# One-hot lookups in every stage of a factor-interaction tower, clears of scratch between gathers, and batches of four units

## The chip, the cores and the metric

The kernel runs on one core of one Trainium2 chip. The metric is the device time of one execution in microseconds (us); lower is better. All data are float32, the ids int32.

## What is computed

A batch of 1024 rows has 32 fields; field f of a row picks a row of 64 numbers from its table. For every pair of fields (p, q) a 64x64 matrix is applied to the first and the product is summed against the second, which gives 496 features. They go, with 16 dense ones, through three layers.

```python
e = jnp.stack([tbl_0[ids[:, 0]], ..., tbl_31[ids[:, 31]]], axis=1)   # 1024 x 32 x 64
p, q = e[:, ROW], e[:, COL]                                          # 496 pairs
kp = jnp.einsum('bpj,ipj->bpi', p, kernel)
z = jnp.sum(kp * q, axis=-1)
h = jnp.concatenate([z, dense_ctx], axis=1)
h = jnp.maximum(h @ W_top1 + b_top1, 0.0)      # 512
h = jnp.maximum(h @ W_top2 + b_top2, 0.0)      # 256
y = h @ W_top3
```

Thirteen of the tables have 1000 rows; the others have 1250, 12500 or 125000.

## The kernel before

Everything is held with the 64 numbers of two fields (a **group**, 16 of them) on the 128 partitions and batch rows on the columns. The batch is worked in four **stages** of 256 rows. A stage has 124 slots of four pairs each (`SLOT`), and two slots are a **unit**: 62 units in a stage, 248 in all. Per unit

- TensorE does four matmuls of 256 columns (`products`, L535) into one of three PSUM buffers `kp`, with the constants in `k_sb`;
- VectorE multiplies the result with the second factor (L481 in one instruction of 1024 columns, or L491 in two of 512) into a ring `prod` of 12 units;
- TensorE sums over partitions with selector matmuls of 32 output rows (`reductions`, L552). They are done per **batch** of units: batches are 5, 6 and 5 units long (`BATCH_UNITS`), and batch b is summed after the fourth unit of batch b+1 (`LAG`).

The groups reach the chip so: GpSimd gathers 128 rows of one table with one indirect DMA (L375); four of them fill one buffer `raw` (a ring of four), two transposes of 128x128 (L519) turn it and ScalarE copies the result from `tr_ps` to `pair` (L393). One such step is an **event**; there are 16 in a stage and 64 in all, and the table `TRANSPOSE_AT` says before which unit each stands in TensorE's program. GpSimd may fill a buffer again when its transposes are done.

Groups 0, 2 and 4 of the first stage are not gathered. Their tables have 1000 rows, so a row is found by a **one-hot lookup**: the table lies on 125 partitions with 8 rows each, VectorE compares the ids, sent to all partitions, with the row numbers (L464, 16 instructions of 256 columns per group), and TensorE multiplies table and one-hot matrix (L511, 16 matmuls of 256 columns per group). The one-hot matrices lie in `prod`, the tables in the end of `k_sb`, which `kd` fills later (L321).

SyncE issues the loads in program order (`load_hot_ids` L332, `load_tables` L338, `load_k` L321) and the copies between partition halves (L329). The loads of the last layers come in the fourth stage. After unit 247 TensorE does the three layers (L573, L579, L586).

In the program each float32 matmul is one instruction; in the trace it is two records with a weight load each, so that a row "x40" is 20 matmuls.

Of the kernel before, what the change touches and what calls it, by code (L numbers as in the profile page):

```python
# [5 lines left out]
I32 = mybir.dt.int32  # L6
# [5 lines left out]
P = 128  # L12
# [13 lines left out]
PROD_RING = 12  # L26
LAG = 4
# [8 lines left out]
BATCH_UNITS = (5, 6, 5)  # L36
# [71 lines left out]
LOOKUP = (0, 2, 4)  # L108
SMALL = 1000
SMALL_P, SMALL_C = 125, 8  # L110
HOT_UNITS = 2 * SMALL_C * WIDTH // (2 * ROWS)

# [7 lines left out]
def unit_slots(u):  # L120
    return range(UNIT[u][1], UNIT[u][1] + UNIT_SLOTS)
# [83 lines left out]
TRANSPOSE_AT = [0, 0, 0, 1, 2, 3, 7, 9, 13, 15, 20, 23, 25, 31, 36, 41, 43, 47, 52, 57, 61, 62, 66, 71, 74, 77, 82,  # L205
                87, 90, 93, 98, 103, 105, 109, 114, 119, 123, 124, 128, 133, 136, 139, 144, 149, 152, 155, 160, 165,
                167, 171, 176, 181, 185, 186, 190, 195, 198, 201, 206, 211, 214, 217, 222, 227]
assert len(TRANSPOSE_AT) == len(EVENT)
assert all(TRANSPOSE_AT[group_event(UNIT[u][0], g)] <= u
           for u in range(UNITS) for s in unit_slots(u) for tile in SLOT[s] for g in groups_of(tile))  # L210

# [20 lines left out]
def pairwise_tower(nc, dense, ids, hot_ids, row_no, tables, kd, ident_in, sel_in, w1, b1, w2, b2, w3, out):  # L232
    from contextlib import ExitStack
    ctx = ExitStack()
    with ctx:
# [3 lines left out]
        def sem(name):  # L239
# [9 lines left out]
        hot_ids_sb = sb("hot_ids_sb", [P, len(LOOKUP), 2, WIDTH], I32)  # L249
# [31 lines left out]
        ids_in = sem("ids_in")  # L281
        consts_in = sem("consts_in")
        row_no_in = sem("row_no_in")
        hot_ids_in = [sem(f"hot_ids_in{i}") for i in range(len(LOOKUP))]
        table_in = [sem(f"table_in{i}") for i in range(len(LOOKUP))]
# [32 lines left out]
        def _(sp):  # L318
# [22 lines left out]
            sp.dma_start(row_sb[0:SMALL_P, :], row_no).then_inc(row_no_in, 16)  # L341
# [6 lines left out]
            for j in range(1, K_AHEAD):  # L348
                load_k(j)
            for u in range(UNITS):  # L350
                st, s = UNIT[u]
                for m in fours_at(u):
                    mix_across(st, m)
                j = s // K_LOAD
# [88 lines left out]
        def _(dve):  # L443
# [14 lines left out]

            dve.wait_ge(row_no_in, 16)
            for i in range(len(LOOKUP)):  # L460
                dve.wait_ge(hot_ids_in[i], 16)
                for c in range(SMALL_C):
                    for n in range(2):
                        nc.vector.tensor_scalar(hot(i, n, c), hot_ids_sb[0:SMALL_P, i, n, :],  # L464
                                                row_sb[0:SMALL_P, c:c + 1], None,
                                                ALU.is_equal).then_inc(hot_ready, 1)
            for u in range(UNITS):
                st, s = UNIT[u]
                if u < PROD_RING and u % HOT_UNITS == 0:

                    dve.wait_ge(transposed, group_event(0, LOOKUP[u // HOT_UNITS]) + 1)
# [14 lines left out]
                else:  # L486
# [7 lines left out]
                    last.then_inc(prod_done, 1)  # L494
            add_dense(LAST)

        @block.tensor
        def _(pe):
            pe.wait_ge(consts_in, 2 * 16)

            def transpose_event(e):
# [169 lines left out]
```

## Time and profile before

| | |
|---|---|
| Time, median of 3 runs | 451.96 us (451.67 to 453.82) |
| Profiled execution: time | 451.3 us |
| Profiled execution: span of its trace | 449.5 us |
| Granted TensorE clock, mean | 0.996 |
| Busy in the span: PE (matmul) | 428.2 us (95%) |
| PEld (weight load) | 283.0 us (63%) |
| DVE (VectorE) | 302.9 us (67%) |
| ACT (ScalarE) | 70.5 us (16%) |
| POOL (GpSimd) | 230.5 us (51%) |

Span is the time from the first to the last instruction of the trace. PE and PEld are the two sides of TensorE. A start time is counted from the start of the span. A chain ("chain that ended last") is followed back from the last instruction, at each step to what released it or to the instruction before it on its engine.

### The profile page before, as it was taken

To read this page: it belongs to the slowest core of one execution; us is meant where nothing else is said; L and a number is where in the kernel's file an instruction comes from. 1 tells how busy PE (TensorE), PEld (TensorE's weight loads), DVE (VectorE), ACT (ScalarE), POOL (GpSimd) and SP (SyncE) were. 2 spreads that over 40 slices of the span, in tenths; PEclk is the share of its full clock that TensorE was granted. 3 is DMA by queue.
4 is the path that set the end of the run, shared out by engine and by line. 5 is a ranking of instruction groups with operands and counts; after the bars stand their busy time and mean duration, and the time that the engine had idled before them with its cause. 6 is when DMAs were issued, how large, how long until landed. Compare 5 with 4: busy or idle time off the path is not lost.

```text
span 449.5 us, 10096 instructions
## 1 busy us (share of the span) xinstructions
PE 428.2 (95%) x4290; PEld 283.0 (63%) x4290; DVE 302.9 (67%) x324; ACT 70.5 (16%) x154; POOL 230.5 (51%) x248
## 2 busy tenths in 40 slices
PE   0769999999999999999999999999999999999997
PEld 0447666767676766767676676767676766664442
DVE  4466687786878686886788787877887787860000
ACT  1002211102021111011221110111211201101122
POOL 4775776556576656565767574747674300000000
PEclk9989999999999999999999999999999999999999
DMA  5663444342111111110111110111151000000000
GB/s 141 199 192 80 126 123 125 100 131 62 22 40 39 25 33 25 20 41 18 39 36 30 29 28 19 39 23 37 31 177 33 14 1 14 1 1 1 0 0 0
DMA packets 15316, 23.55 MB, mean 52 GB/s; under 512 B 5505, under 2 KB 7809, under 8 KB 15144
## 3 DMA queue, kind: packets, MB, share of 16 engines
q1 hardware_dynamic: 6884, 14.14, 10.4%
q0 software_dynamic: 7808, 8.01, 9.3%
q10 hardware_dynamic: 580, 0.76, 0.6%
q8 instruction: 34, 0.56, 0.5%
q14 instruction: 10, 0.08, 0.1%
HBM read 20.79 MB, written 0.00 MB: 46 GB/s over the span
## 4 chain that ended last, share of the span: by engine, by line
PE 95%; DMA 3%; issue 1%; ACT 0%; SPq 0%
PE kp L535 52%; PE z_ps L552 25%; PE kp L573 6%; PE tr_ps L519 5%; PE tr_ps L511 3%; PE kp L579 3%; DMA k_sb<-in_tbl 3%; PE kp L586 0%; ACT pair L393 0%; ACT prod L437 0%; SPq L332 0%; SPq L338 0%; SPq L341 0%
## 5 line engine op out<-in xcount | busy, mean ns | idle before, releaser
L481 DVE TENSOR_TENSOR prod<-kp,pair 128x1024 f32<-128x1024 f32 x224 | 259.0, 1216 | 83.9 <-PE kp L535 83.9
L375 POOL DMA_INDIRECT raw<-in_tbl,ids_sb x244 | 230.3, 944 | 122.1 <-issue 67.0
L535 PE MATMUL kp<-pair,k_sb 64*128 64x256 f32 x1984 | 238.8, 387 | 0.0
L535 PEld LDWEIGHTS kp<-pair,k_sb 64*128 64x128 f32 x1984 | 182.9, 187 | 41.9 <-DVE prod L481 11.3
L552 PE MATMUL z_ps<-prod,ones_sel 128*32 128x256 f32 x1984 | 117.0, 382 | 0.0
L552 PEld LDWEIGHTS z_ps<-prod,ones_sel 128*32 128x32 f32 x1984 | 59.7, 110 | 50.5 <-issue 10.7
L393 ACT ACTIVATE pair<-tr_ps 128x256 f32<-128x256 f32 x64 | 24.5, 383 | 247.4 <-PE tr_ps L519 218.6
L511 PE MATMUL tr_ps<-prod,k_sb 125*64 125x256 f32 x96 | 14.3, 464 | 17.9 <-DMA k_sb<-in_tbl 13.4
L491 DVE TENSOR_TENSOR prod<-kp,pair 128x512 f32<-128x512 f32 x48 | 30.0, 681 | 0.0
L573 PE MATMUL kp<-z_sb,k_sb 128*128 128x512 f32 x64 | 28.0, 596 | 0.0
L519 PEld LDWEIGHTS tr_ps<-ident,raw 128*128 128x128 f32 x122 | 12.3, 141 | 24.2 <-issue 23.3
L519 PE MATMUL tr_ps<-ident,raw 128*128 128x128 f32 x122 | 26.7, 301 | 0.5 <-ACT pair L393 0.5
L464 DVE TENSOR_SCALAR prod<-hot_ids_sb,row_sb 125x256 f32<-125x256 int32 x48 | 14.8, 383 | 15.0 <-DMA hot_ids_sb<-in_hot_ids 8.5
L511 PEld LDWEIGHTS tr_ps<-prod,k_sb 125*64 125x64 f32 x96 | 9.6, 169 | 22.0 <-issue 18.5
L573 PEld LDWEIGHTS kp<-z_sb,k_sb 128*128 128x128 f32 x64 | 12.0, 190 | 15.1 <-issue 15.1
L405 ACT ACTIVATE pair<-pair 64x512 f32<-64x512 f32 x32 | 20.1, 628 | 0.8
L411 ACT ACTIVATE z_sb<-z_ps 128x256 f32<-128x256 f32 x12 | 4.6, 383 | 69.3 <-PE z_ps L552 69.3
L404 ACT ACTIVATE pair<-pair 64x256 f32<-64x256 f32 x32 | 13.1, 408 | 7.1 <-DVE prod L491 6.7
L579 PE MATMUL kp<-prod,k_sb 128*128 128x512 f32 x32 | 13.9, 593 | 0.0
L431 ACT ACTIVATE prod<-kp,b_sb 128x512 f32<-128x512 f32 x8 | 5.5, 687 | 37.5 <-PE kp L573 19.3
L579 PEld LDWEIGHTS kp<-prod,k_sb 128*128 128x128 f32 x32 | 6.1, 190 | 7.6 <-issue 7.6
L448 DVE TENSOR_TENSOR z_sb<-z_ps,z_sb 128x256 f32<-128x256 f32 x4 | 1.7, 416 | 5.5 <-PE z_ps L552 5.5
(9 smaller groups left out, 7.4 us busy)
## 6 DMA issues: line engine op xcount, KB each, us to landing
k_sb<-in_kd SPq DMA_DIRECT2D x15, 512.0 KB, 4.1
raw<-in_tbl,ids_sb POOLq DMA_INDIRECT x244
pair<-pair SPq DMA_DIRECT2D x32, 64.0 KB, 2.3
k_sb<-in_tbl SPq DMA_DIRECT2D x6, 250.0 KB
k_sb<-in_w SPq DMA_DIRECT2D x1, 1024.0 KB
hot_ids_sb<-in_hot_ids SPq DMA_DIRECT2D x3, 250.0 KB
z_sb<-in_dense ACTq DMA_DIRECT2D x1, 512.0 KB, 8.8
k_sb<-in_w SPq DMA_DIRECT2D x1, 512.0 KB
```

Of the source, the lines that this page charges most:

```text
L375: nc.gpsimd.indirect_dma_start(raw[:, r % RAW_RING, i, n, :], None, tables[f], bass.IndirectOffsetOnAxis(ap=ids_sb[:, 2 * b + i, f:f + 1], ...
L393: nc.scalar.activation(pair[:, group_place(st, k):group_place(st, k) + n, :], tr_ps[:, 0:n * WIDTH].rearrange("p (n w) -> p n w", n=n), AC ...
L405: nc.scalar.activation(pair[both, a:b + 1:b - a, :], pair[both, k + 1:k + 2, :].broadcast_to([64, 2, WIDTH]), ACT.Copy).then_inc(mixed_cop ...
L464: nc.vector.tensor_scalar(hot(i, n, c), hot_ids_sb[0:SMALL_P, i, n, :], row_sb[0:SMALL_P, c:c + 1], None, ALU.is_equal).then_inc(hot_ready, 1)
L481: nc.vector.tensor_tensor(prod[:, u % PROD_RING, :, :].rearrange("p q (i n) -> p (q i) n", i=UNIT_SLOTS), kp[u % KP_RING][:, :, :].rearran ...
L491: last = nc.vector.tensor_tensor(prod[:, u % PROD_RING, :, i * WIDTH:(i + 1) * WIDTH], kp[u % KP_RING][:, :, i * WIDTH:(i + 1) * WIDTH], p ...
L511: last = nc.tensor.matmul(tr_ps[64 * i:64 * i + 64, 0:WIDTH], table_sb[0:SMALL_P, lookup, i, c, :], hot(lookup, i, c), start=(c == 0), sto ...
L519: last = nc.tensor.transpose(tr_ps[:, to:to + P], raw[:, r % RAW_RING, i, :, :].rearrange("p a n -> p (a n)"), ident[:, :])
L535: last = nc.tensor.matmul(kp[u % KP_RING][:, q, i * WIDTH:(i + 1) * WIDTH], k_sb[rows, x, :], pair[rows, group_place(st, owner // 2), :], ...
L552: last = nc.tensor.matmul(z_ps[32 * g:32 * g + 32, :], ones_sel[:, 30 - col:62 - col], prod[:, u % PROD_RING, q, i * WIDTH:(i + 1) * WIDTH ...
L573: last = nc.tensor.matmul(dst[:, 0, :], w1_sb[:, c, n * P:(n + 1) * P], z_sb[:, c, h * ROWS:(h + 1) * ROWS], start=(c == 0), stop=(c == FC ...
L579: last = nc.tensor.matmul(dst[:, 0, :], w2_sb[:, c, n * P:(n + 1) * P], h1_sb[:, h, c, :], start=(c == 0), stop=(c == N1 - 1))
```

## The change

- `LOOKUP` is now a list of ten (stage, group) pairs: groups 0, 2, 4 and 6 of the first stage, groups 2 and 6 of each other stage. 216 gathers are left of 244 (54 buffers instead of 61).
- Tables and row numbers are padded to 128 partitions; the two tables of a group come in one DMA from a new array `small`. The one-hot matrix of a group is made by 8 instructions of 512 columns. That of the third lookup and of the six late ones lies in a new tile `hot_sb`, that of the fourth in `z_sb`. All four early ones are made before VectorE's first product; the late ones behind single units (`hot_units`).
- The two late tables and the dense features are loaded at unit 24 (`DENSE_AT`).
- The ids come in two loads; GpSimd's first gathers need the first only.
- GpSimd clears a scratch tile of 128x576 float32 four times behind every four gathers, each clear waiting for the one before (`rest`).
- Batches are 4, 4, 4, 4 units, `LAG` is 3, the ring `prod` is 8 units instead of 12.
- `TRANSPOSE_AT` is a new table.

```diff
-PROD_RING = 12
-LAG = 4
+PROD_RING = 8
+LAG = 3
-BATCH_UNITS = (5, 6, 5)
+BATCH_UNITS = (4, 4, 4, 4)
-LOOKUP = (0, 2, 4)
-SMALL_P, SMALL_C = 125, 8
+LOOKUP = ((0, 0), (0, 2), (0, 4), (0, 6), (1, 2), (1, 6), (2, 2), (2, 6), (3, 2), (3, 6))
+EARLY = 4
+SMALL, SMALL_C = 1000, 8
+BURST, REST, REST_COLS = 4, 4, 576
+DENSE_AT = 24
...
-TRANSPOSE_AT = [0, 0, 0, 1, 2, 3, 7, 9, 13, 15, 20, 23, 25, 31, 36, 41, 43, 47, 52, 57, 61, 62, 66, 71, 74, 77, 82,
+TRANSPOSE_AT = [0, 0, 0, 1, 2, 4, 7, 10, 11, 17, 23, 27, 31, 39, 43, 47, 51, 55, 62, 63, 64, 66, 69, 72, 73, 79, 85,
...
+def hot_units(i):
+
+    end = TRANSPOSE_AT[look_event(i)] - 1
+    first = max(end - 2 * SMALL_C, TRANSPOSE_AT[look_event(i - 1)] + 1)
+    return [first + c * (end - first) // SMALL_C for c in range(SMALL_C)]
...
             def load_tables(i):
-                for n in range(2):
-                    table = tables[2 * LOOKUP[i] + n].rearrange("(p c) e -> p c e", c=SMALL_C)
-                    sp.dma_start(table_sb[0:SMALL_P, i, n, :, :], table).then_inc(table_in[i], 16)
+                sp.dma_start(early_table_sb[:, i, :, :, :], small[:, i, :, :, :]).then_inc(table_in[i], 16)
...
             load_hot_ids(2)
             load_tables(2)
-            for j in range(1, K_AHEAD):
+            load_k(1)
+            load_hot_ids(3)
+            load_tables(3)
+            for j in range(2, K_AHEAD):
                 load_k(j)
...
+            def rest(n):
+                for i in range(REST):
+                    if n or i:
+                        pool.wait_ge(rested, REST * n + i)
+                    nc.gpsimd.memset(rest_sb[:, :], 0.0).then_inc(rested, 1)
...
+                        done = 4 * r + 2 * i + n + 1
+                        if done % BURST == 0 and done < 4 * len(GATHER):
+                            rest(done // BURST - 1)
...
-            act.dma_start(ids_sb[:, :, :], ids).then_inc(ids_in, 16)
+            act.dma_start(ids_sb[:, 0:WIDTH // P, :], ids[:, 0:WIDTH // P, :]).then_inc(ids_in, 16)
...
-            act.dma_start(z_sb[:, FC - 1, :], dense).then_inc(dense_in, 16)
+            act.dma_start(ids_sb[:, WIDTH // P:, :], ids[:, WIDTH // P:, :]).then_inc(ids_rest_in, 16)
...
+            def make_hot(i, c):
+                if c == 0:
+                    dve.wait_ge(hot_ids_in[i % EARLY], (i // EARLY + 1) * 16)
+                    if i >= EARLY:
+
+                        dve.wait_ge(transposed, look_event(i - 1 if i > EARLY else 2) + 1)
+                nc.vector.tensor_scalar(hot(i, c), hot_ids_sb[:, i % EARLY, :], row_sb[:, c:c + 1], None,
+                                        ALU.is_equal).then_inc(hot_ready, 1)
...
-            for i in range(len(LOOKUP)):
-                dve.wait_ge(hot_ids_in[i], 16)
+            for i in range(EARLY):
                 for c in range(SMALL_C):
...
+                    make_hot(i, c)
...
                     last.then_inc(prod_done, 1)
+                for i, c in hots_behind(u):
+                    make_hot(i, c)
```

TensorE's program from its start, before the change. `tr_ps<-prod,k_sb` is a lookup, `tr_ps<-ident,raw` a pair of transposes, `kp` the products (x4 is one unit), `z_ps` a batch's sums:

```order
L511 MATMUL tr_ps<-prod,k_sb 64x256 x16
L519 MATMUL tr_ps<-ident,raw 128x128 x2
L511 MATMUL tr_ps<-prod,k_sb 64x256 x16
L535 MATMUL kp<-pair,k_sb 128x256 x4
L519 MATMUL tr_ps<-ident,raw 128x128 x2
L535 MATMUL kp<-pair,k_sb 128x256 x4
L511 MATMUL tr_ps<-prod,k_sb 64x256 x16
L535 MATMUL kp<-pair,k_sb 128x256 x4
```

Up to here both programs are alike but for the unit behind the third lookup. From there, with the change (`tr_ps<-z_sb,k_sb` is the lookup of group 6):

```order
L582 MATMUL tr_ps<-hot_sb,k_sb 64x256 x16
L606 MATMUL kp<-pair,k_sb 128x256 x8
L590 MATMUL tr_ps<-ident,raw 128x128 x2
L606 MATMUL kp<-pair,k_sb 128x256 x12
L623 MATMUL z_ps<-prod,ones_sel 32x256 x16
L582 MATMUL tr_ps<-z_sb,k_sb 64x256 x16
L606 MATMUL kp<-pair,k_sb 128x256 x12
```

The first sums stand behind unit 6 instead of unit 8, and a fourth lookup follows them.

TensorE around the start of the second stage (unit 62), before the change:

```order
L552 MATMUL z_ps<-prod,ones_sel 32x256 x12
L519 MATMUL tr_ps<-ident,raw 128x128 x2
L535 MATMUL kp<-pair,k_sb 128x256 x20
L552 MATMUL z_ps<-prod,ones_sel 32x256 x20
L519 MATMUL tr_ps<-ident,raw 128x128 x2
L535 MATMUL kp<-pair,k_sb 128x256 x12
```

and with the change, from unit 62 to the lookup before unit 69:

```order
L582 MATMUL tr_ps<-hot_sb,late_table_sb 64x256 x16
L606 MATMUL kp<-pair,k_sb 128x256 x4
L590 MATMUL tr_ps<-ident,raw 128x128 x2
L606 MATMUL kp<-pair,k_sb 128x256 x4
L590 MATMUL tr_ps<-ident,raw 128x128 x2
L606 MATMUL kp<-pair,k_sb 128x256 x4
L623 MATMUL z_ps<-prod,ones_sel 32x256 x8
L606 MATMUL kp<-pair,k_sb 128x256 x4
L590 MATMUL tr_ps<-ident,raw 128x128 x2
L606 MATMUL kp<-pair,k_sb 128x256 x12
L623 MATMUL z_ps<-prod,ones_sel 32x256 x16
L582 MATMUL tr_ps<-hot_sb,late_table_sb 64x256 x16
```

Two lookups stand where transposes stood, and the runs of units between them are shorter. The other two stage starts look the same.

VectorE with the change, at the same stage start (L547 and L557 are the products, L526 the one-hot comparisons, L509 the dense features of the stage before). Before the change there is no comparison behind the first 48:

```order
L526 TENSOR_SCALAR hot_sb<-hot_ids_sb,row_sb 128x512 x2
L547 TENSOR_TENSOR prod<-kp,pair 128x1024
L526 TENSOR_SCALAR hot_sb<-hot_ids_sb,row_sb 128x512 x2
L509 TENSOR_TENSOR z_sb<-z_ps,z_sb 128x256
L547 TENSOR_TENSOR prod<-kp,pair 128x1024
L526 TENSOR_SCALAR hot_sb<-hot_ids_sb,row_sb 128x512
L547 TENSOR_TENSOR prod<-kp,pair 128x1024
L526 TENSOR_SCALAR hot_sb<-hot_ids_sb,row_sb 128x512 x2
L547 TENSOR_TENSOR prod<-kp,pair 128x1024
L526 TENSOR_SCALAR hot_sb<-hot_ids_sb,row_sb 128x512
```

Eight comparisons lie behind five units here; those of the lookup at unit 62 lie two units apart.

## Rows read from the trace of the kernel before

**Rows 1.** Page: the chain that ended last, by line.

```profile
PE kp L535 52%; PE z_ps L552 25%; PE kp L573 6%; PE tr_ps L519 5%; PE tr_ps L511 3%; PE kp L579 3%; DMA k_sb<-in_tbl 3%; PE kp L586 0%; ACT pair L393 0%; ACT prod L437 0%; SPq L332 0%; SPq L338 0%; SPq L341 0%
```

**Rows 2.** Windows: length; busy of PE, PEld, DVE, ACT, POOL; clock, DMA share, GB/s.

```profile
0.00:5.00 5.00, 0.00 (x0) 0.00 (x0) 0.00 (x0) 1.28 (x1) 0.27 (x5) 1.00 0.40 91
5.00:10.00 5.00, 0.00 (x0) 0.00 (x0) 3.51 (x12) 0.00 (x0) 3.84 (x4) 1.00 0.59 179
...
20.00:25.00 5.00, 4.67 (x40) 3.34 (x41) 0.86 (x4) 0.43 (x2) 3.78 (x4) 1.00 0.86 246
...
30.00:35.00 5.00, 4.65 (x28) 3.43 (x30) 2.10 (x2) 0.00 (x0) 3.78 (x4) 0.66 0.39 129
...
120.00:180.00 60.00, 60.00 (x670) 41.23 (x668) 46.47 (x46) 10.92 (x25) 40.51 (x43) 1.00 0.15 32
```

**Rows 3.** The chain in order of time: start, length, what.

```profile
26.50 3.84 issue
...
37.14 3.65 PE kp L535 x32
43.09 2.29 PE z_ps L552 x40
...
62.19 2.79 PE kp L535 x24
...
69.95 5.86 PE kp L535 x48
75.81 2.73 PE z_ps L552 x48
78.90 4.73 PE kp L535 x40
...
401.80 3.63 PE kp L573 x8
```

**Rows 4.** Timeline of PE: start, length, line, what.

```profile
102.29 0.44 PE L519 MATMUL tr_ps<-ident,raw 128*128 128x128 f32 x2
102.66 4.80 PE L535 MATMUL kp<-pair,k_sb 64*128 64x256 f32 x40
```

**Rows 5.** Timeline of the first 36 us.

```profile
13.40 5.31 PE L511 MATMUL tr_ps<-prod,k_sb 125*64 125x256 f32 x32 [13.40 <-DMA k_sb<-in_tbl]
...
20.33 3.67 PE L511 MATMUL tr_ps<-prod,k_sb 125*64 125x256 f32 x32 [0.70 <-ACT pair L393]
...
23.94 1.14 PE L535 MATMUL kp<-pair,k_sb 64*128 64x256 f32 x8
...
24.77 5.07 DVE L464 TENSOR_SCALAR prod<-hot_ids_sb,row_sb 125x256 f32<-125x256 int32 x16 [4.14 <-DMA hot_ids_sb<-in_hot_ids]
...
30.35 5.36 PE L511 MATMUL tr_ps<-prod,k_sb 125*64 125x256 f32 x32 [3.84 <-issue]
```

**Rows 6.** Groups by shape: count, busy us, mean ns, idle time before.

```profile
L481 DVE TENSOR_TENSOR prod<-kp,pair 128x1024 f32<-128x1024 f32 x224 | 259.0, 1216 | 83.9 <-PE kp L535 83.9
...
L491 DVE TENSOR_TENSOR prod<-kp,pair 128x512 f32<-128x512 f32 x48 | 30.0, 681 | 0.0
...
L405 ACT ACTIVATE pair<-pair 64x512 f32<-64x512 f32 x32 | 20.1, 628 | 0.8
...
L404 ACT ACTIVATE pair<-pair 64x256 f32<-64x256 f32 x32 | 13.1, 408 | 7.1 <-DVE prod L491 6.7
```

**Rows 7.** Timeline of GpSimd: a clear of one column and a gather.

```profile
0.33 0.12 POOL L660 MEMSET const-uint8-127<- 128x1 uint8 x1
...
8.81 0.94 POOL L375 DMA_INDIRECT raw<-in_tbl,ids_sb  x1 [0.30 <-issue]
```

**Rows 8.** Waits: who for whom, us in total, times, longest.

```profile
POOL raw L375 <- PE tr_ps L519: 50.6, 24, 2.8
```

**Rows 9.** Page: DMA issues, KB each, us to landing.

```profile
pair<-pair SPq DMA_DIRECT2D x32, 64.0 KB, 2.3
...
z_sb<-in_dense ACTq DMA_DIRECT2D x1, 512.0 KB, 8.8
```

More of the change, by code:

```diff
@@ L103, in groups_of @@
     return [owner // 2, factor] if m is None else [owner // 2, 2 * m, 2 * m + 1]
-LOOKUP = (0, 2, 4)
-SMALL = 1000
-SMALL_P, SMALL_C = 125, 8
+LOOKUP = ((0, 0), (0, 2), (0, 4), (0, 6), (1, 2), (1, 6), (2, 2), (2, 6), (3, 2), (3, 6))
+EARLY = 4
+SMALL_GROUPS = tuple(k for st, k in LOOKUP[:EARLY])
+LATE_GROUPS = tuple(k for st, k in LOOKUP[EARLY:EARLY + 2])
+assert all(LOOKUP[i][1] == LATE_GROUPS[i % 2] for i in range(EARLY, len(LOOKUP)))
+SMALL, SMALL_C = 1000, 8
 HOT_UNITS = 2 * SMALL_C * WIDTH // (2 * ROWS)
+BURST, REST, REST_COLS = 4, 4, 576
+DENSE_AT = 24
 UNIT_SLOTS = ROWS // WIDTH
@@ L229, in dense_row, with pairwise_tower @@
     return 32 * (n // (32 - used)) + used + n % (32 - used)
-def pairwise_tower(nc, dense, ids, hot_ids, row_no, tables, kd, ident_in, sel_in, w1, b1, w2, b2, w3, out):
+def pairwise_tower(nc, dense, ids, hot_ids, row_no, small, tables, kd, ident_in, sel_in, w1, b1, w2, b2, w3, out):
     from contextlib import ExitStack
@@ L281, in pairwise_tower @@
         ids_in = sem("ids_in")
+        ids_rest_in = sem("ids_rest_in")
         consts_in = sem("consts_in")
         row_no_in = sem("row_no_in")
-        hot_ids_in = [sem(f"hot_ids_in{i}") for i in range(len(LOOKUP))]
-        table_in = [sem(f"table_in{i}") for i in range(len(LOOKUP))]
+        hot_ids_in = [sem(f"hot_ids_in{i}") for i in range(EARLY)]
+        table_in = [sem(f"table_in{i}") for i in range(EARLY)]
+        late_tables_in = sem("late_tables_in")
+        rested = sem("rested")
         hot_ready = sem("hot_ready")
@@ L353, in _ @@
                     mix_across(st, m)
+                for i in range(EARLY, len(LOOKUP)):
+                    if u == hot_units(i)[0] - 6:
+                        sp.wait_ge(hot_ready, SMALL_C * (i - EARLY + 1))
+                        sp.wait_ge(kp_done, u + 1)
+                        load_hot_ids(i)
+                if u == DENSE_AT:
+                    sp.wait_ge(kp_done, u + 1)
+                    sp.dma_start(z_sb[:, FC - 1, :], dense).then_inc(dense_in, 16)
+                    for n, k in enumerate(LATE_GROUPS):
+                        sp.dma_start(late_table_sb[:, n, :, :, :],
+                                     small[:, SMALL_GROUPS.index(k), :, :, :]).then_inc(late_tables_in, 16)
                 j = s // K_LOAD
@@ L506, in transpose_event @@
                 if lookup is not None:
-                    pe.wait_ge(table_in[lookup], 2 * 16)
+                    if lookup < EARLY:
+                        pe.wait_ge(table_in[lookup], 16)
+                    else:
+                        pe.wait_ge(late_tables_in, len(LATE_GROUPS) * 16)
                     for c in range(SMALL_C):
+                        pe.wait_ge(hot_ready, SMALL_C * lookup + c + 1)
                         for i in range(2):
-                            pe.wait_ge(hot_ready, 2 * (SMALL_C * lookup + c) + i + 1)
-                            last = nc.tensor.matmul(tr_ps[64 * i:64 * i + 64, 0:WIDTH],
-                                                    table_sb[0:SMALL_P, lookup, i, c, :], hot(lookup, i, c),
+                            last = nc.tensor.matmul(tr_ps[64 * i:64 * i + 64, 0:WIDTH], table(lookup, i, c),
+                                                    hot(lookup, c)[:, i * WIDTH:(i + 1) * WIDTH],
                                                     start=(c == 0), stop=(c == SMALL_C - 1), skip_group_check=True)
@@ L611 @@
     tables = [_np.asarray(inputs[f"tbl_{f}"]) for f in range(FIELDS)]
-    small = [f for f in range(FIELDS) if tables[f].shape[0] == SMALL][:2 * len(LOOKUP)]
+    small = [f for f in range(FIELDS) if tables[f].shape[0] == SMALL][:2 * EARLY]
     others = [f for f in range(FIELDS) if f not in small]
-    field_at = [small.pop(0) if i // 2 in LOOKUP else others.pop(0) for i in range(FIELDS)]
+    field_at = [small.pop(0) if i // 2 in SMALL_GROUPS else others.pop(0) for i in range(FIELDS)]
     tables = [tables[f] for f in field_at]
+    small = _np.zeros((2 * EARLY, P * SMALL_C, EMBED), _np.float32)
+    for i in range(EARLY):
+        for n in range(2):
+            small[2 * i + n, 0:SMALL] = tables[2 * SMALL_GROUPS[i] + n]
+    small = small.reshape(EARLY, 2, P, SMALL_C, EMBED).transpose(2, 0, 1, 3, 4)
     pair_no = {}
@@ L654 @@
     sel[64:128, 31] = 1.0
-    arrays = {"dense": dense_rows, "ids": ids, "hot_ids": hot_ids, "row_no": row_no, "ident": _np.eye(P, dtype=_np.float32), "sel": sel}
+    arrays = {"dense": dense_rows, "ids": ids, "hot_ids": hot_ids, "row_no": row_no, "small": small, "ident": _np.eye(P, dtype=_np.float32), "sel": sel}
     for f in range(FIELDS):
@@ L666 @@
     out = nc.dram_tensor("out_y", (HALVES, ROWS), _mybir.dt.float32, kind="ExternalOutput").ap()
-    pairwise_tower(nc, ap["dense"], ap["ids"], ap["hot_ids"], ap["row_no"], [ap[f"tbl_{f}"] for f in range(FIELDS)], ap["kd"],
+    pairwise_tower(nc, ap["dense"], ap["ids"], ap["hot_ids"], ap["row_no"], ap["small"], [ap[f"tbl_{f}"] for f in range(FIELDS)], ap["kd"],
                    ap["ident"], ap["sel"], ap["w1"], ap["b1"], ap["w2"], ap["b2"], ap["w3"], out)
```

53 lines of the change are left out of this document (32 added, 21 removed).

## The prediction

> **What bounds the kernel now.** I read the chain that ended last first: products are 52% of the span, sums 25%, the layers 9%, transposes 5% and lookups 3%, all of it TensorE's, and the table load that the first lookup waits for is 3% [rows 1]. Then the windows: between 120 and 180 us TensorE is busy 60.00 of 60.00 us at a granted clock of 1.00, VectorE 46.5, GpSimd 40.5 [rows 2]. GpSimd waits 50.6 us for transposes to free a buffer [rows 8], so gathers run ahead of TensorE. In the steady part nothing but TensorE's own instructions counts. The start is different: the first sums begin at 43.09 us, the last layers at 401.80 [rows 3], and ahead of 43 us TensorE waits for tables and ids.
>
> **Prices on TensorE.** A run of three units takes 2.79 us, of four 3.65, of five 4.73, of six 5.86 [rows 3]. So a run costs 0.86 us a unit and 0.21 at its end; the fifth unit adds 0.22 more and the sixth brings that to 0.49. VectorE, with 1.22 us per unit against TensorE's 0.86 [rows 6], is then no longer hidden by three buffers. A batch of five units is summed in 2.29 us, one of six in 2.73 [rows 3]: 0.109 per matmul and 0.12, so 1.86 for four units. A pair of transposes is 0.37 (102.29 to 102.66) [rows 4]. A lookup at the full clock takes 3.61 us (20.33 to 23.94) [rows 5].
>
> I check these prices on the kernel before, counting its program from the first sums to the layers: they add to 358.6 us, and the trace has 401.80 - 43.09 = 358.7 [rows 3]. They can be trusted.
>
> **The change on TensorE.** Seven pairs of transposes become lookups: 7 x (3.61 - 0.37) = +22.7 us. Nothing hides them, since TensorE has no idle time to put them in.
> Batches of four: the products stand in 83 runs instead of 65 (18 x 0.21 = +3.8), but none is longer than four units (27 runs of five and 2 of six lose 27 x 0.22 + 2 x 0.49 = 6.9): -3.1 us. The sums ahead of the layers stand in 63 groups instead of 47 (16 x 0.12 = 1.9) and hold one unit more, since the batch left over for the layers has two units instead of three (0.4): +2.4. Together -0.7; the batches pay next to nothing.
> In all TensorE's program ahead of the layers goes from 379.7 to 401.6 us. From the first sums on the new one has 382.8 us.
>
> **The start.** Where do the first sums begin now (S)? They come two units earlier in the program. The first table was there at 13.4 [rows 5]. By 10 us the DMA engines had moved 5 x (91 + 179) GB/s = 1.35 MB [rows 2]; the 0.52 MB of dense features [rows 9] and 0.1 MB of ids now come later, and at 0.18 to 0.25 MB per us that is 2.5 to 3.4 us. So the first lookup begins at about 10.3. From its start to that of the second took 6.93 us (it runs slower than the others, 5.31), and from there to the point where unit 1 is done 6.17 (20.33 to 26.50) [rows 3, 5]: 23.4. Here the kernel before stood 3.84 us for its third table, and the lookup then took 5.36 us, at a granted clock of 0.66 over that window [rows 2, 3, 5]. The new program has less ahead of this table and only one load of constants behind it that shares the engines, so I take both away: the third lookup ends at 27.0, and five units with a pair of transposes (2 x 0.86 + 0.21 + 0.37 + 2.79 = 5.1) end at 32.1.
> VectorE now has four lookups to prepare before its first product. Sixteen comparisons of 256 columns take 5.07 us [rows 5], 0.31 each, and a column costs (1216 - 681) / 512 = 1.04 ns [rows 6], so one of 512 takes 0.57 and 32 take 18.3 us. Without waits they would be ready at 25; the fourth ids come behind about 4.4 MB, which is 21 us at 246 GB/s [rows 2] and 25 at 200, so it will be 26 to 30. In the late case unit 3 waits for the product of unit 0, and S is 35. So S is 30.6 to 35; I take 32.5, 10.6 us earlier than before.
> The Trainium skill (DMA: Bandwidth & Descriptors, on why a DMA increments its semaphore by 16) says that a transfer is split over the largest number up to 16 that divides its outer dimensions; that is 5 engines for 125 partitions and 16 for 128. The DMA share of 0.40 and 0.59 in the first windows and 0.86 in the later one agrees [rows 2]. By the rule the tables would come faster than I reckon, S would be near 29 and the time about 462.
>
> **VectorE.** Six late lookups put 48 x 0.57 = 27 us on VectorE. It has 13.5 us free in 60 [rows 2]. Its products take 289 us for 248 units, 1.17 each [rows 6]. Where comparisons lie two units apart, four units need 4 x 1.17 + 2 x 0.57 = 5.8 us against TensorE's 5.51 (3.65 + 1.86), or 5.88 with transposes: level. Around unit 65 eight comparisons lie behind five units: from unit 62 to 68 VectorE needs 12.7 us, TensorE 11.0 with two sums and three pairs of transposes. The 1.7 us are made up during the lookup that follows (3.61 us with no product to do). I take 2 us in all, bounded by 0 and 8. Were that lookup not there to cover, three places would cost 5.
> The smaller ring is free: a batch is summed three units into the next one, and VectorE needs its places only for the fifth unit.
>
> **GpSimd.** A gather goes by every 1.25 us, 0.94 busy and 0.30 in the sequencer [rows 7]. 216 of them take 269.5 us, from 4.9 on, and with 2 us to land (a copy between partitions takes 2.3 [rows 9]) the last would be there at 276.4. Between them lie 53 x 4 = 212 clears of 576 columns, m each. The last transposes stand before unit 233, and behind their beginning TensorE has 21.6 us up to the layers, so they are due at 394. GpSimd keeps up if 276.4 + 212 m is below 394: m up to 0.55 us. If the sequencer prepares the next gather during the last clear of four, 0.30 is hidden 53 times, and m may be 0.63.
> What is m? The trace has no such clear. The lower bound is a clear of one column, 0.12 us [rows 7]. For the rate there are only other engines: 0.86 ns per column on ScalarE ((628 - 408) / 256) and 1.04 on VectorE [rows 6]. With the fixed part that is 0.62 to 0.72, and each clear waits for the one before. This is just where GpSimd becomes the bound. I take 0.62, ScalarE's rate, with the sequencer's time hidden: 7.2 us for four gathers and four clears, at the limit, and it costs nothing. The bounds are 0 and, with m = 0.72 and nothing hidden, a time of 276.4 + 153 + 21.6 + 47.3 + 1.8 = 500. m = 0.65 gives 485, or 469 hidden; m = 0.72 hidden 484.
> The Trainium skill (GPSIMD Engine Reference, Elementwise: side-by-side cycle accounting) has 1.03 cycles per element at 1.2 GHz for simple bodies, an estimate of 0.49 us for 576 and 0.6 with a fixed part. That would leave the sum as it is if the sequencer's time is hidden and give 474 if not. No row of this trace shows it.
>
> **Sum.** The layers begin at 32.5 + 382.8 + 2.0 = 417.3. From there the trace before has 47.7 us, now 0.4 less for the smaller last batch. Span 464.6; the profiled time was 1.8 over the span (451.3 against 449.5; the median of the runs is 451.96), so 466.4: **466 us**, 3.2% slower.
>
> **Rivals.**
> 1. GpSimd becomes the bound: 470 to 500, 485 at m = 0.65. For it speaks VectorE's rate; against it the hidden sequencer time, and that a clear reads nothing. It decides from m = 0.55 to 0.63 on.
> 2. The other side, no change or faster: the start. TensorE needs 382.8 + 47.3 + 1.8 = 431.9 us from the first sums on, so S must be below 22.3 us for a time within 0.5% of before and below 17.8 to be faster by more. Ahead of S stand 18.8 us of TensorE's work at full clock, 1.7 more for the slow first lookup and some 1.5 of copies: 22 us, and the first table would have to be there at 0.3 us.
> 3. VectorE costs its upper bound, 8 us: 472.
> 4. The loads at unit 24 (1.6 MB ahead of a load of constants that is due 12 units, 17 us, later) make TensorE wait. 2.1 MB at 0.2 MB per us is 10.5 us, so it is hidden; at half that rate it costs 4 us: 470.
>
> **How the numbers follow.** My forecast, TensorE the bound (459 to 470): 0.60. GpSimd the bound above 470: 0.30. Rivals 3 and 4: 0.06. Rival 2: 0.04, most of it "no change". 0.5% is about what a measurement of this kernel tells from none. The range reaches down below S = 28 without VectorE's term (460) and up to m = 0.65 with nothing hidden (485); some 0.15 lies beyond. So 459 to 485; faster 0.01, same 0.03, slower 0.96.
>
> **What would show it.** Ten lookups of 3.6 us, in sum 36 to 38, and 54 pairs of transposes. The first sums at 30 to 35 us. Products in runs of four at 3.65. GpSimd: a clear's mean, four gathers and four clears in 7.2 us or less, no transposes that wait for a gather. VectorE's comparisons at 0.6 us, and no wait for it over 1 us behind the start. The prediction is wrong if TensorE has gaps in front of transposes behind 100 us, or if the first sums begin before 29.

## The result

The changed kernel takes 484.47 us (median of 4 runs, 483.67 to 485.33) against 451.81 for the kernel before in the same comparison: 1.0721 times as long, 95% interval 1.0672 to 1.0771. The profiled execution has a span of 482.1 us. The forecast was 466 us; the time is inside the range (459 to 485), but more than twice as far above the kernel before as forecast (33 us, not 14). The first rival named 485 for m = 0.65; what was measured is m = 0.625, and the agreement with 485 is luck (see the failed step below).

Page of the changed kernel: busy time, the chain that ended last, and three groups:

```profile
PE 457.0 (95%) x4500; PEld 298.4 (62%) x4500; DVE 329.4 (68%) x356; ACT 70.7 (15%) x154; POOL 335.4 (70%) x432
...
POOL raw L433 26%; PE kp L606 22%; POOL rest_sb L422 15%; PE z_ps L623 11%; PE kp L644 6%; PE kp L650 3%; DMA raw<-in_tbl,ids_sb 3%; PE tr_ps L582 2%; PE tr_ps L590 2%; DMA ids_sb<-in_ids 1%; PE kp L657 0%; ACT prod L498 0%; POOLq L429 0%
...
L433 POOL DMA_INDIRECT raw<-in_tbl,ids_sb x216 | 208.6, 966 | 63.0 <-issue 57.2
...
L422 POOL MEMSET rest_sb<- 128x576 f32 x212 | 126.8, 598 | 9.2
...
L590 PE MATMUL tr_ps<-ident,raw 128*128 128x128 f32 x108 | 23.8, 302 | 14.2 <-DMA raw<-in_tbl,ids_sb 14.1
```

The busy share of TensorE says nothing, 95% in both. The chain says it at once: all TensorE before [rows 1], now 41% of the span are gathers and clears. The wait of GpSimd for transposes, 50.6 us before [rows 8], is 0.5, and instead TensorE's transposes wait 14.1 us for gathers, in 12 places. One period of GpSimd and one such place in the timeline:

```profile
199.62 2.50 POOL L422 MEMSET rest_sb<- 128x576 f32 x4
...
202.28 0.95 POOL L433 DMA_INDIRECT raw<-in_tbl,ids_sb  x1 [0.16 <-issue]
...
203.53 0.94 POOL L433 DMA_INDIRECT raw<-in_tbl,ids_sb  x1 [0.30 <-issue]
...
238.76 0.66 PE L590 MATMUL tr_ps<-ident,raw 128*128 128x128 f32 x2 [2.50 <-DMA raw<-in_tbl,ids_sb]
...
239.35 5.49 PE L606 MATMUL kp<-pair,k_sb 64*128 64x256 f32 x24
```

Four clears take 2.50 us, 0.625 each. The gap ahead of the gather behind them is 0.16 instead of 0.30, so half of the sequencer's time is hidden, not all. From clear to clear it is 7.35 us where nothing disturbs (199.62 to 206.97, the start of the next clears). The last row is slow as well: three units take 5.42 us up to the start of the sums instead of 2.79 [rows 3]. The granted clock was 1.00 from 232 to 236 us, and 0.76 and then 0.50 in the windows that hold and follow the wait of 2.5 us; 0.50 is its level of 1.2 GHz (windows; the columns are those of [rows 2]):

```profile
232.00:236.00 4.00, 4.00 (x42) 2.33 (x38) 3.79 (x5) 1.43 (x4) 3.08 (x4) 1.00 0.13 26
236.00:240.00 4.00, 1.50 (x10) 0.86 (x8) 3.47 (x6) 0.52 (x2) 3.66 (x5) 0.76 0.08 16
240.00:244.00 4.00, 4.00 (x22) 3.23 (x20) 2.46 (x4) 0.90 (x2) 2.94 (x4) 0.50 0.11 21
```

### The profile page after: what moved, and what is told of

Read it like the earlier page. It is cut to its first block, busy times and chain, and to the rows that moved or that the text cites. A ratio compares the mean times of both kernels' runs of the same rounds, so it can differ in the third digit from the quotient of the medians.

```text
span 482.1 us, 10756 instructions
## 1 busy us (share of the span) xinstructions
PE 457.0 (95%) x4500; PEld 298.4 (62%) x4500; DVE 329.4 (68%) x356; ACT 70.7 (15%) x154; POOL 335.4 (70%) x432
## 4 chain that ended last, share of the span: by engine, by line
PE 47%; POOL 41%; issue 8%; DMA 4%; ACT 0%; POOLq 0%
POOL raw L433 26%; PE kp L606 22%; POOL rest_sb L422 15%; PE z_ps L623 11%; PE kp L644 6%; PE kp L650 3%; DMA raw<-in_tbl,ids_sb 3%; PE tr_ps L582 2%; PE tr_ps L590 2%; DMA ids_sb<-in_ids 1%; PE kp L657 0%; ACT prod L498 0%; POOLq L429 0%
## 5 line engine op out<-in xcount | busy, mean ns | idle before, releaser
L547 DVE TENSOR_TENSOR prod<-kp,pair 128x1024 f32<-128x1024 f32 x224 | 262.4, 1217 | 100.3 <-PE kp L606 100.1
L433 POOL DMA_INDIRECT raw<-in_tbl,ids_sb x216 | 208.6, 966 | 63.0 <-issue 57.2
L606 PEld LDWEIGHTS kp<-pair,k_sb 64*128 64x128 f32 x1984 | 186.6, 189 | 42.0 <-issue 15.4
L422 POOL MEMSET rest_sb<- 128x576 f32 x212 | 126.8, 598 | 9.2
L623 PE MATMUL z_ps<-prod,ones_sel 128*32 128x256 f32 x1984 | 120.4, 382 | 0.0
L590 PE MATMUL tr_ps<-ident,raw 128*128 128x128 f32 x108 | 23.8, 302 | 14.2 <-DMA raw<-in_tbl,ids_sb 14.1
L526 DVE TENSOR_SCALAR hot_sb<-hot_ids_sb,row_sb 128x512 f32<-128x512 int32 x56 | 31.4, 583 | 0.0
L557 DVE TENSOR_TENSOR prod<-kp,pair 128x512 f32<-128x512 f32 x48 | 30.0, 680 | 0.0
L582 PE MATMUL tr_ps<-hot_sb,late_table_sb 128*64 128x256 f32 x192 | 22.0, 382 | 0.0
L582 PE MATMUL tr_ps<-prod,k_sb 128*64 128x256 f32 x64 | 12.6, 579 | 8.1 <-DMA ones_sel<-in_sel 7.6
L582 PEld LDWEIGHTS tr_ps<-hot_sb,late_table_sb 128*64 128x64 f32 x192 | 13.3, 137 | 8.5 <-issue 2.5
L582 PEld LDWEIGHTS tr_ps<-prod,k_sb 128*64 128x64 f32 x64 | 6.7, 212 | 13.5 <-DMA ones_sel<-in_sel 7.6
L526 DVE TENSOR_SCALAR prod<-hot_ids_sb,row_sb 128x512 f32<-128x512 int32 x16 | 8.2, 586 | 5.7 <-DMA row_sb<-in_row_no 5.7
```

The costliest lines, as they stand in the source:

```text
L422: nc.gpsimd.memset(rest_sb[:, :], 0.0).then_inc(rested, 1)
L433: nc.gpsimd.indirect_dma_start(raw[:, r % RAW_RING, i, n, :], None, tables[f], bass.IndirectOffsetOnAxis(ap=ids_sb[:, 2 * b + i, f:f + 1], ...
L526: nc.vector.tensor_scalar(hot(i, c), hot_ids_sb[:, i % EARLY, :], row_sb[:, c:c + 1], None, ALU.is_equal).then_inc(hot_ready, 1)
L547: nc.vector.tensor_tensor(prod[:, u % PROD_RING, :, :].rearrange("p q (i n) -> p (q i) n", i=UNIT_SLOTS), kp[u % KP_RING][:, :, :].rearran ...
L557: last = nc.vector.tensor_tensor(prod[:, u % PROD_RING, :, i * WIDTH:(i + 1) * WIDTH], kp[u % KP_RING][:, :, i * WIDTH:(i + 1) * WIDTH], p ...
L590: last = nc.tensor.transpose(tr_ps[:, to:to + P], raw[:, r % RAW_RING, i, :, :].rearrange("p a n -> p (a n)"), ident[:, :])
```

## One table for the runs

Each row is a run whose edit is below; e5 to e8 ran on another chip and are left out. S is the start of the first sums, "layers" that of the last layers, both in us. "Counted" is its TensorE program from the first sums to the layers by the prices of the prediction; "measured" the same stretch of its trace, whose two ends are S and the start of the layers.

| kernel | S | layers | measured | counted | time |
|---|---|---|---|---|---|
| before | 43.1 | 401.8 | 358.7 | 358.6 | 451.8 |
| changed | 35.0 | 434.8 | 399.8 | 382.8 | 484.5 |
| e9 changed again | 39.4 | 440.9 | 401.5 | 382.8 | 489.9 |
| e15 changed, third time | 34.1 | 436.1 | 402.0 | 382.8 | 482.8 |
| e1 no clears | 33.6 | 416.8 | 383.2 | 382.8 | 465.9 |
| e10 no clears again | 38.0 | 421.2 | 383.2 | 382.8 | 470.4 |
| e2 three clears | 34.6 | 419.4 | 384.8 | 382.8 | 468.0 |
| e3 early lookups only | 34.7 | 398.1 | 363.4 | 363.4 | 447.4 |
| e4 before, four clears | 41.1 | 484.5 | 443.4 | 358.6 | 534.0 |
| e11 three early lookups | 36.5 | 396.6 | 360.2 | 360.1 | 444.0 |
| e12 before, 128 partitions | 33.2 | 391.9 | 358.7 | 358.6 | 443.2 |
| e13 before, batches of four | 40.1 | 404.7 | 364.6 | 364.8 | 455.3 |
| e14 as e12, dense late | 36.2 | 394.9 | 358.7 | 358.6 | 444.2 |
| e16 before, one clear | 40.8 | 399.4 | 358.7 | 358.6 | 451.7 |

Only the kernels with three or four clears leave the count by more than 0.4 us. S is not as steady: the same kernel has it at 34.1, 35.0 and 39.4 us, and the one without clears at 33.6 and 38.0. Why is shown in the section on what the hardware did.

## The experiments

**Clears away, and one fewer.** e1 drops the call of `rest`; e2 is

```diff
-BURST, REST, REST_COLS = 4, 4, 576
+BURST, REST, REST_COLS = 4, 3, 576
```

> The changed kernel without the clears between gathers, all else as it is. Theory A (four gathers and four clears take 7.35 us, more than the 7.17 that TensorE leaves, so GpSimd became the bound): TensorE waits for no gather behind the start, the first sums stay at about 35 us, and the time is 35.0 + 382.8 + 47.3 + 1.8 = 467, at most 469. Theory B (the late lookups cost more than their matmuls, by VectorE or by the clock): it stays above 475.

> The changed kernel with three clears behind four gathers instead of four. Theory A: a period of 4.99 + 3 x 0.625 - 0.14 = 6.7 us, below the limit of 7.17, so the time is that without clears, 467. If the clears cost in proportion (theory C: each clear adds on the path, not only beyond a limit), three quarters of the loss of some 17 us stay and the time is about 480.

e1: 465.87 us, ratio 1.0327 (1.0309 to 1.0344). e2: 468.0, 1.0376 (1.0349 to 1.0402). So the fourth clear alone is worth 16 us and the first three together about 2, which is less than e1 and e10, the same kernel, lie apart: a threshold, as theory A has it, and not a price per clear (C). e2 is 2.0 us over its count and waits for no gather behind the first sums. Most of that (0.8 and 0.9 us) lies in the units from 131 and from 330 us on, where comparisons and products stand close together on VectorE and TensorE waits 0.57 and 0.66 us for a product. In e1 TensorE waits for one gathered group only, the first:

```profile
POOL raw L433 <- PE tr_ps L587: 104.9, 39, 10.5
...
PE tr_ps L587 <- DMA raw<-in_tbl,ids_sb: 3.5, 1, 3.5
```

GpSimd again waits for TensorE, for 104.9 us. The same kernel once more, e10 below, gave 470.36; its S is 38.0, and from there on it needs 383.2 us again.

**Late lookups away.** e3 takes the six late lookups and the clears out:

```diff
-LOOKUP = ((0, 0), (0, 2), (0, 4), (0, 6), (1, 2), (1, 6), (2, 2), (2, 6), (3, 2), (3, 6))
+LOOKUP = ((0, 0), (0, 2), (0, 4), (0, 6))
```

> The changed kernel with the four lookups of the first stage only and no clears: the six late ones are gathered and transposed again. By the price of a lookup (3.61 - 0.37 us each): 6 x 3.24 = 19.4 less than without clears, 447.5, which is 1% below the kernel before. If the late lookups cost more than that (comparisons on VectorE that TensorE waits for), it is lower still, down to 440; if the kernel with shorter runs and a tight gather schedule waits elsewhere, it is at or above 452.

447.35 us, 0.9911 (0.9889 to 0.9932): 0.9% faster than the kernel before. That is 18.5 us less than e1 for six lookups; from the first sums to the layers it is 19.8, against 19.4 counted.

**Clears alone.** e4 puts the four clears into the kernel before.

```diff
+                if r + 1 < len(GATHER):
+                    for i in range(4):
+                        if r or i:
+                            pool.wait_ge(rested, 4 * r + i)
+                        nc.gpsimd.memset(rest_sb[:, :], 0.0).then_inc(rested, 1)
```

> The kernel before with four clears of 576 columns behind every four gathers and nothing else. Theory A: 61 buffers at 7.35 us from 4.9 us on, the last one there at 453, then 30.5 us of units and sums, 47.7 of layers and 1.8: 533. If clears are hidden when TensorE is the bound (theory C reversed: GpSimd catches up in its waits of 50.6 us only), it is 452 + 60 x 2.36 - 50.6 = 543 at most; below 500 both are wrong.

534.03 us, in one run only. Clears cost 83 us here (451.06 in the same comparison), with 61 buffers to bring instead of 54; transposes wait 64.8 us for gathers in 31 places. GpSimd's schedule alone, 61 buffers at 7.35 us, had given 533.

**Four kernels on another chip.** The next four ran on a chip where the kernel before took 531.53 us in the median of 13 runs, so their ratios stand for that chip only.

```diff
-BATCH_UNITS = (5, 6, 5)
+BATCH_UNITS = (4, 4, 4, 4)
-LAG = 4
+LAG = 3
```

is e5, in the kernel before. e6 and e7 are e3 with `LOOKUP` and `EARLY` cut to three and two pairs. e8 gives the kernel before the new loads of the tables (the array `small` that they read is left out here); the edit does two things, tables on 128 partitions and one load for two tables:

```diff
-SMALL_P, SMALL_C = 125, 8
+SMALL_P, SMALL_C = 128, 8
...
-                for n in range(2):
-                    table = tables[2 * LOOKUP[i] + n].rearrange("(p c) e -> p c e", c=SMALL_C)
-                    sp.dma_start(table_sb[0:SMALL_P, i, n, :, :], table).then_inc(table_in[i], 16)
+                sp.dma_start(table_sb[:, i, :, :, :], small[:, i, :, :, :]).then_inc(table_in[i], 16)
```

> The kernel before with batches of four units and sums three units behind, its transpose table and ring as they are. By the prices of the prediction its products stand in 105 runs (before 65) and its sums in 63 groups: TensorE's program gets 3.9 us longer ahead of the layers, 0.4 shorter behind: 454.5. If batches are a gain by themselves (shorter runs keep VectorE out of the way, ends of runs cost nothing) it is 445 to 449.

> The changed kernel without late lookups and clears, and with group 6 of the first stage gathered too, so three lookups as before. One lookup less by its price: 447.4 - 3.2 = 444.1, if GpSimd, which has one more group to bring in the first 40 us, stays ahead (group 8 is due at about 41 us and should land at 40). If it doesn't, or if the fourth lookup was free because TensorE waited there anyway, 447.

> The same with two lookups, groups 0 and 2. TensorE's program is 3.2 us shorter again, but the seventh gathered group is due at about 38 us and can't land before 45 at 5 us each: GpSimd bounds the start, 446 to 449. If gathers are no bound at the start, 441.

> The kernel before with tables, ids for the lookups and row numbers on 128 partitions instead of 125, the two tables of a group in one load; all else as it is. Theory A: the loads on 125 partitions use few DMA engines, and that made the old start late. Then the first table is there at 8 instead of 13.4 us, the stop of 3.8 us ahead of the third lookup goes with its slow clock, the first sums come at about 35.5 instead of 43.1, and the time is 444. Theory B: the dense features and the amount of data set it: then it stays within 2 us of 451.

e5: 513.41, 0.9676 (0.9602 to 0.975). e6: 539.66, 1.0163 (1.0091 to 1.0236). e7: 540.7, 1.0157 (1.0086 to 1.0227). e8: 529.3, 0.996 (0.9917 to 1.0004). None of the forecast times holds there, and the ratios are not those of the other chips: the same edits gave 1.0075 (e13 for e5), 0.9816 (e11 for e6) and 0.9811 (e12 for e8) later; e7 was not run again. What differs is seen in e6's timeline of TensorE around the last gather, which starts at 440.19 us:

```profile
402.13 2.50 PE L617 MATMUL z_ps<-prod,ones_sel 128*32 128x256 f32 x32
...
405.62 0.91 PE L600 MATMUL kp<-pair,k_sb 64*128 64x256 f32 x3
...
406.87 0.70 PE L600 MATMUL kp<-pair,k_sb 64*128 64x256 f32 x3 [0.33 <-issue]
...
408.98 5.27 PE L600 MATMUL kp<-pair,k_sb 64*128 64x256 f32 x26 [1.41 <-issue]
...
447.86 3.72 PE L600 MATMUL kp<-pair,k_sb 64*128 64x256 f32 x32
...
451.51 1.93 PE L617 MATMUL z_ps<-prod,ones_sel 128*32 128x256 f32 x32
...
453.74 3.73 PE L600 MATMUL kp<-pair,k_sb 64*128 64x256 f32 x32
```

While gathers run TensorE stops in the middle of a run with nothing to wait for in the profile; behind the last one it keeps the old pace (3.65 us to the next start). So on that chip gathers coincide with a TensorE that starves. That they cause it is argued from this ordering only. All four kernels have it: behind the last gather they leave the count by 0.8 us or less, ahead of it by 51 to 91.

**Again, where the kernel before takes 451.7 us.** e9 is the changed kernel, e10 is e1, e11 is e6 and e12 is e8.

> The changed kernel once more. In the last four runs the kernel before took 531 us instead of 451; in their traces TensorE starves and its signals come 1.4 us late, until GpSimd's last gather (at 412 or 441 us), and behind it runs of four units take 3.65 us again. Theory D: where gathers disturb TensorE, time is set by their number and density, and the changed kernel (216 gathers for 244, a clear of 2.4 us between fours) is faster than before: 490 to 515 against 531. Where they don't (before at 451) it is 484 again. Theory E: the disturbance is not the gathers'; then the change costs its 33 us there too, 560.

> The changed kernel without clears once more. Where gathers disturb TensorE: theory D puts it above the one with clears if density counts (505 to 530), and at or below it if only the number of gathers counts, since the clears bound GpSimd. Where they don't: 466 again.

> Three early lookups, no late ones, no clears, once more. Where gathers don't disturb TensorE: 444.1, as written before, or 447 if the fourth lookup was free. Where they do: 540 again, above the kernel before, since its gathers are as many.

> The kernel before with tables, lookup ids and row numbers on 128 partitions, once more. Where gathers don't disturb TensorE: first sums at about 35.5 us and 444 if the 125 partitions held the loads back, within 2 of 451 if not. Where they do: 529 again.

e9: 489.89 us, 1.078 (1.0708 to 1.0852), with S at 39.4; from there it needs 401.5 us, near the 399.8 of the first time. e10: 470.36, 1.0402 (1.0346 to 1.0457). e11: 443.99, 0.9816 (0.9794 to 0.9838), and e12: 443.2, 0.9811 (0.9792 to 0.983), both as expected for such a chip; S of e12 is 33.2, where 35.5 was expected. e12 against the kernel before is all in the start: the first lookup begins at 7.2 instead of 13.4, and the third follows the second unit at once and takes 3.67 us instead of 5.36 [rows 5]. The edit also makes one load of two, and no run parts that from the 128 partitions.

```profile
7.22 5.69 PE L509 MATMUL tr_ps<-prod,k_sb 128*64 128x256 f32 x32 [7.22 <-DMA ones_sel<-in_sel]
...
15.18 0.41 PE L517 MATMUL tr_ps<-ident,raw 128*128 128x128 f32 x2 [2.27 <-DMA raw<-in_tbl,ids_sb]
...
22.17 3.67 PE L509 MATMUL tr_ps<-prod,k_sb 128*64 128x256 f32 x32
```

**The last four.** e13 is e5 once more, e15 the changed kernel; e14 is e12 with the dense features loaded at unit 24 from SyncE; e16 is e4 with `range(1)`.

> The kernel before with batches of four and nothing else, once more. Where the kernel before takes 451: counted, 3.9 us more ahead of the layers and 0.4 less behind, 454.5; at or below 450 the prices of the ends of runs are wrong. Where it takes 531: 513 again.

> The kernel before with tables on 128 partitions and the dense features loaded at unit 24. In the kernel with the tables alone TensorE waits 2.3 us for the first gathered group, behind 1.7 MB of loads. With 0.5 MB less ahead it lands earlier: 1 to 2.3 us off, 441 to 442. If the gathers' landing hangs on the tables and constants instead, 443.

> The changed kernel a third time. Where the kernel before takes 451: 484 to 490. Where it takes 531: theory D 490 to 515, theory E 560.

> The kernel before with one clear behind four gathers, 5.5 us for both. Where it takes 451: below the limit of about 6.2 us at which GpSimd would bound it, so no change, 451 to 452.5. Where it takes 531: below 531 if the density of gathers is what disturbs TensorE, 531 if only their number is.

e13: 455.28, 1.0075 (1.0048 to 1.0102), as counted. e14: 444.21, 0.9812 (0.9749 to 0.9875): no gain over e12 where 1 to 2.3 us were expected, the first transposes still wait 2.30 us for their gather. e15: 482.76, 1.0663 (1.0601 to 1.0725). e16: 451.66, 0.999 (0.9966 to 1.0014): a clear below the limit is free. None of e9 to e16 ran on a chip as slow as that of e5 to e8, so what they were to show there stays open.

## Why the prediction was wrong

**The step that failed** is the term of GpSimd: "I take 0.62, ScalarE's rate, with the sequencer's time hidden: 7.2 us for four gathers and four clears, at the limit, and it costs nothing." The clear was sized well, 0.625 us from start to start in the timeline against 0.62. Two things in the step were wrong: that all of 0.30 is hidden behind the clears (0.14 is), and that nothing else delays GpSimd.

How late GpSimd is can be read at the last gather that TensorE waits for, the fourth of buffer 48:

```profile
362.87 5.61 DMA raw<-in_tbl,ids_sb
...
368.62 0.41 PE tr_ps L590 x2
```

By the prediction's terms this gather is issued at 4.9 + 47 x 7.2 + 3 x 1.25 = 347.05 us; it was issued at 362.87, 15.8 later. Of these

- 7.0 are the period where nothing disturbs, 47 x (7.35 - 7.2);
- 4.2 are the first two buffers, which took 8.8 and 10.1 us; one gather in them took 3.26;
- 3.7 are the 18 periods in the stretches with late comparisons, 7.35 to 7.95 us each;
- 0.9 is the start, at 5.81 us instead of 4.9.

The gather then took 5.6 us to land where others take 2.5, while the weights of the layers come in (DMA share 0.80 at 271 GB/s from 364 to 368 us). By the count the transposes of this buffer are due at 352.0 us (their place in e1, moved by the 1.4 us between the two S), and by the prediction's schedule the gather would have landed 2.3 us before that. So they start 15.8 + 3.1 - 2.3 = 16.6 us late, at 368.6. That is the 17.0 us between measured (399.8) and counted (382.8), but for 0.4. None of the last six buffers is waited for. So the prediction set the due time of the last buffer only, and the ones that bind lie before it: each 0.1 us of period costs 47 times that here, 4.7 us.

That GpSimd sets the time up to there is seen from its own side: from its first gather at 5.8 us on it never stands idle for more than 0.31 us at a time, which is the gap that every gather has. Seen from TensorE, the 17.0 us are 11.6 of waits behind 20 us (14.1 less 2.5 in front of the first transposes), 0.9 for starting again behind them, and 4.5 of slow instructions, 2.6 of them behind the wait at 236 us and 1.7 behind one of 1.9 us at 341 us, where the clock fell again:

```profile
344.00:348.00 4.00, 4.00 (x28) 3.02 (x28) 3.64 (x6) 0.76 (x2) 2.97 (x4) 0.59 0.12 21
```

The slow instructions are no cause beside the gathers: TensorE would have waited that much longer for buffer 48.

The first rival had the right engine, but not this sum. With the measured clear and the measured hidden part it gives 276.4 + 212 x 0.625 - 53 x 0.14 + 21.6 + 47.3 + 1.8 = 472; the other 12 us are delays that it didn't have either. Putting a value at such an edge on the free side made nothing out of a term of 16 us, and the chance of 0.30 for the other side was too small.

**Right:**
- TensorE's prices and the count. In eight kernels without a GpSimd limit the stretch behind the first sums is within 0.4 us of the count. The six late lookups cost what was counted (e1 against e3), so nothing hid them, and batches of four moved with a new transpose table pay nothing. Alone with the old table they cost 3.5 us (e13).
- The sum without clears: 466.4 forecast, 465.9 (e1) and 470.4 (e10) measured.
- VectorE costs TensorE next to nothing without clears: e1's stretch is 0.4 us over the count, 2 were allowed. What the prediction didn't have is that VectorE's comparisons delay GpSimd (above, and below).
- The loads at unit 24 are hidden.

**Half right:** the start. S came at 35.0, the late end of the 30.6 to 35, and at 34.1 and 39.4 when the kernel ran again. But the reason given (VectorE late with four lookups) is not the one. The first lookup began at 7.65 us, earlier than the 10.3 reckoned from bytes, and the fourth comparisons were done at 20.7. Between its first two lookups TensorE waited 2.5 us for the first gathered group, and both ran slowly, 6.2 and 6.4 us; the granted clock was 0.62 from 15 to 20 us. e12 has the same wait, shorter, and its second lookup takes 3.67. In e9 the wait is 8.5 us and in e10 7.3, and that is their late S.

For the loads, the rule of the Trainium skill on the number of DMA engines (DMA: Bandwidth & Descriptors, why a DMA increments its semaphore by 16) was the better guide. The rows of the changed kernel agree, against a DMA share of 0.59 at 179 GB/s before [rows 2]:

```profile
5.00:10.00 5.00, 2.35 (x12) 1.41 (x14) 4.26 (x11) 0.00 (x0) 3.58 (x3) 1.00 1.01 355
10.00:15.00 5.00, 3.85 (x24) 1.91 (x20) 5.00 (x8) 0.38 (x1) 4.36 (x6) 1.00 1.04 395
```

For S it was not: the prediction drew 29 from it, and no run of the changed kernel had it before 34.1: the tables came sooner, but TensorE then waited for the first gathered group.

## What to carry to other kernels

A background engine that works at a period under what the critical engine leaves is free (e16, and but for 2 us e2), and one just over it costs the difference times all periods up to the last one that is waited for; so where an estimate ends near such an edge, forecast both sides with their prices and not the free one. Set the due time of every buffer and not only of the last, and ask which other engine can delay the background one. Price the critical engine by runs and their ends from start to start, and check the sum on the kernel at hand: here it gave eight kernels within 0.4 us. And take a change apart: this one holds a gain of 8 us (the new loads of the tables, e12) under 22 us of lookups and some 17 us of clears; e12 at 443.2 us and e11 at 444.0 beat both kernels.

## What the hardware did that I had not expected

**Comparisons of 512 columns hold up gathers.** Timeline of GpSimd and VectorE in the changed kernel, with one window, and below the same in e9, where the comparisons before these run without a gap from 5.75 us on:

```profile
17.43 3.25 DVE L526 TENSOR_SCALAR z_sb<-hot_ids_sb,row_sb 128x512 f32<-128x512 int32 x8
17.54 3.26 POOL L433 DMA_INDIRECT raw<-in_tbl,ids_sb  x1 [0.30 <-issue]
19.00:20.00 1.00, 1.00 (x6) 0.49 (x6) 1.00 (x4) 0.00 (x0) 1.00 (x1) 0.50 0.00 0
```

```profile
8.73 9.98 POOL L433 DMA_INDIRECT raw<-in_tbl,ids_sb  x1 [0.30 <-issue]
...
15.35 3.25 DVE L526 TENSOR_SCALAR z_sb<-hot_ids_sb,row_sb 128x512 f32<-128x512 int32 x8
```

The gather takes 3.26 us in one and 9.98 in the other, instead of 0.94, and ends 0.11 and 0.12 us behind the last comparison. It is not the loads: from 19 to 20 us no DMA runs. Ten of the traces have comparisons of 512 columns. In seven (e2, e3, e10, e11 and e15 too) one gather took 3.3 to 10.0 us and ended 0.11 to 0.12 us behind the last of the early comparisons; in the other three (e1, e6, e7) gathers among them took up to 1.28 us. In the eight with comparisons of 256 columns no gather took over 1.08 us. Whether it happens, and to which gather, differs from run to run of the same kernel: in e9 and e10 it is one of the first buffer, for which TensorE then waits 8.5 and 7.3 us, in the changed kernel and in e15 one of the second, and in e1 none. S and the time differ with it. No run changes the width of the comparisons alone, so the cause is argued from these rows.

**A comparison of 512 columns is quicker than its columns suggested, and it and a clear slow one another.** Timeline of VectorE without clears (e1) and, below, of the changed kernel:

```profile
199.56 0.48 DVE L523 TENSOR_SCALAR hot_sb<-hot_ids_sb,row_sb 128x512 f32<-128x512 int32 x1
...
202.22 0.47 DVE L523 TENSOR_SCALAR hot_sb<-hot_ids_sb,row_sb 128x512 f32<-128x512 int32 x1
```

```profile
205.12 0.48 DVE L526 TENSOR_SCALAR hot_sb<-hot_ids_sb,row_sb 128x512 f32<-128x512 int32 x1
...
206.97 2.66 POOL L422 MEMSET rest_sb<- 128x576 f32 x4
...
207.78 0.71 DVE L526 TENSOR_SCALAR hot_sb<-hot_ids_sb,row_sb 128x512 f32<-128x512 int32 x1
```

Eight in a row take 3.24 us in e1, 0.41 each, where 0.57 was reckoned from 1.04 ns a column. The comparison that meets clears takes 0.71 (up to 0.95 elsewhere in this kernel) and the four clears 2.66 instead of 2.50; in e4, which has no late comparisons, no clear is longer than 0.627 us, and in the changed kernel the longest is 0.868. Gathers in these stretches take up to 1.15 us for 0.94. The Trainium skill (SBUF — State Buffer, Who interferes with whom) says that a `tensor_scalar` in a 2-port mode and GpSimd lock each other out. The rows agree that they hold one another up, gathers too; whether these comparisons run in such a mode no row says, only that 512 columns take 0.41 us where 256 take 0.31.

**The clock can fall behind a wait under 2 us, and need not behind a longer one.** In the changed kernel the granted clock was at its lower level behind the waits of 2.5 us (to 238.8) and 1.9 us (to 342.9), and not behind the one of 1.5 us to 216.1, where four units took 3.65 us as ever. In e15 it fell behind a wait of 1.8 us (to 368.3; 0.65 from 370 to 374 us, and two units took 3.0 us instead of 1.93) and stayed at 1.00 behind one of 2.4 us (to 343.5), and in e9 it stayed at 1.00 behind 2.4 us (to 244.2). So the length of the wait alone doesn't tell.

**Chips differ.** One chip took 531.5 us for a kernel that takes 451.7 on the others, with gaps in TensorE up to the last gather. Whether it is the gathers that cause them, and whether the changed kernel's fewer and sparser gathers pay there, stays open: the changed kernel wasn't run on it.
